# Four cross-attention layers on one core: a narrow job's sixteen heads of scores in one group of plain float32 products, into four PSUM banks

## The chip, the cores and the metric

The kernel runs on one core of one Trainium2 chip. The metric is the device time of one execution in microseconds; three executions of a kernel are shown and their median is what is compared. One more execution was recorded by the hardware profiler, and all rows below come from it. TensorE (PE in the rows) multiplies, VectorE (DVE), ScalarE (ACT) and GpSimd (POOL) work elementwise, SyncE (SP) issues DMAs. PEld is TensorE's loading of the stationary operand.

## The reference, cut to what matters

```python
# x: (8, 128, 128); ctx: (8, 128, 256). Layers 0 and 3 (narrow): 16 heads of width 8 over 4 key/value heads, RMS norm
inv = rsqrt(mean(x * x, -1) + 1e-5)
q = (x * inv * norm_w) @ wq                # (B, T, 16, 8), seen as (B, T, g=4, r=4, 8)
k, v = ctx @ wk, ctx @ wv                  # (B, S, g=4, 8)
attn = softmax(einsum('btgrd,bsgd->bgrts', q, k) / sqrt(8))
x = x + einsum('bgrts,bsgd->btgrd', attn, v).reshape(B, T, 128) @ wo
# Layers 1 and 2 (wide): 16 heads of width 64, own keys and values per head, no norm
logits = einsum(q, k) * 64 ** -0.5 + col_bias       # two or four columns suppressed by a mask
x = x + softmax(logits) @ v @ Wo + bo
```

The result must agree with float32 arithmetic. A product of float32 operands runs on TensorE as two instructions ("hi" and "lo" passes over the same columns; every such matmul appears twice in the counts). Operands of type float32r run in one pass at lower precision; where the kernel before uses them, it splits a number into a rounded part and a rest and sums three products.

## The kernel before

**Jobs and halves.** A job is one layer for one of the eight batches: 32 jobs, in the order of `JOBS`. Jobs 0 to 3, 12 to 15, 16 to 19 and 28 to 31 are narrow (layers 0, 3, 0, 3), the sixteen others wide. Each job has two halves, o = 2n + h, of eight heads ("octet"), and each octet two sides of four heads, one PSUM bank of 128 x 512 each. All engines step through the same halves, each with a hand-written order (`half` in each block): in half o, TensorE makes the scores of octet o, transposes the probabilities of octet o-2, multiplies the values of octet o-3, makes the products of the context that the table `FILLS` names for this half (keys and values of later jobs, one bank each), the queries of the next job and, in even halves, the output projection of job n-2. VectorE reads the scores and writes them negated with a running minimum (L615, four instructions per side), takes reciprocals of the sums (L622), copies transposed probabilities (L626) and outputs (L631, L633) out of PSUM. ScalarE takes the exponentials (L482, four per side), copies one side's transposes in narrow jobs (L499), and copies every fill (L468) and the wide queries (L474). GpSimd normalises (L379).

**Banks.** Two banks `scores_ps`, two `pt_ps` for transposes, two `fill_ps` used in turn by all fills (`fill_bank`), one `v_ps` (values, output, mean square), one `q_ps` (queries). A half's scores can be written only when VectorE has read those of the half before; from octet 57 on, after the last fill, the odd octets take the two fill banks instead (`scores_bank`).

**A narrow job's scores.** The four key heads of width 8 stand as 32 rows; `diagonal_keys` (L334) spreads them into a block form of 4 x 128 columns, so that one product of 512 columns gives four heads' scores. Precision comes from a stack of three such parts (`STACK` = 96 rows): rounded query with rounded key, rest of the query, rest of the key, in float32r, one pass. `queries` (L788) makes the stacked query for four r's by four products; `narrow_queries` on VectorE rounds it (L594) and takes the rest (L598), both over 512 columns; `split_keys` on GpSimd (`first_keys_rest` on VectorE for the first) rounds the keys. `scores` (L825) then runs two products of 512 columns in each half.

**Things that the steps touch.** `fill_out` on ScalarE copies a fill after `exponentials(o, 1)`, in half o for the first name of a half and at the start of half o+1 for the second. `weighted_values` waits for `rms_out` of a job whose mean square shares the bank. `mean_out` (L586) is the first step of the narrow norm on VectorE, right after `add_input` at the start of an odd half.

```python
scores:  pe.wait_ge(scores_read[side], m + 1)    # m: the octet before in these banks
         nc.tensor.matmul(out[side][:], qn[0:STACK, n % 2, 2 * h + side, :], keys, ...)
```

## Time and profile before

| | us |
|---|---|
| three runs, median (lowest to highest) | 380.88 (380.61 to 384.76) |
| the profiled execution's own time | 380.89 |
| its span, first to last instruction | 379.1 |
| TensorE / VectorE / ScalarE / GpSimd busy | 359.7 / 267.7 / 279.0 / 187.6 |

The profiled execution lies within 0.01 us of the median, and 1.79 us of it lie outside the span. Narrow jobs' scores are made from 10.1 to 48.3, from 159.6 to 235.5 and from 333.3 to 366.1 us; between these stretches lie the wide jobs.

### The profile page before, as it was taken

The page shows a single profiled execution, that of the slowest core. Times are in us where ns is not written, and L with a number is a line of the kernel's source. Part 1 is how long each engine was busy: PE and PEld are TensorE (multiplying, and loading weights), DVE is VectorE, ACT ScalarE, POOL GpSimd, SP SyncE. Part 2 cuts the span into 40 slices and gives each one's busy share as a digit, 9 for nine tenths or more (in the row PEclk, how much of TensorE's full clock was granted, in tenths as well). Part 3 has the DMA queues.
Part 4 walks back from the last instruction along what each step waited for, and adds up shares of the span by engine and source line. Part 5 has one row for each costly group of instructions (what it writes and reads, how often), then busy time and mean ns, then how long its engine had stood idle before and what let it go on. Part 6 is the DMA issues. An engine that isn't in the chain of part 4 may idle for free.

```text
span 379.1 us, 10494 instructions
## 1 busy us (share of the span) xinstructions
PE 359.7 (95%) x3522; PEld 319.1 (84%) x3522; DVE 267.7 (71%) x1401; ACT 279.0 (74%) x1176; POOL 187.6 (49%) x220
## 2 busy tenths in 40 slices
PE   8889999999999999999999999999999999978665
PEld 8787799899999998889889988888999989867554
DVE  2999975636536547696978886577564785699982
ACT  4889998865665567475899999998566865647793
POOL 3677853733223236454676765443333435447662
PEclk9899999999999999999999999999999999999979
DMA  7925000000000000000000000000000000000000
GB/s 232 411 66 216 1 3 3 2 3 2 1 2 3 2 0 3 2 3 0 10 3 9 9 8 2 3 3 2 0 3 2 3 2 1 2 3 3 7 9 14
DMA packets 4883, 9.91 MB, mean 26 GB/s; under 512 B 608, under 2 KB 3296, under 8 KB 4576
## 3 DMA queue, kind: packets, MB, share of 16 engines
q1 hardware_dynamic: 4400, 8.91, 6.5%
q8 instruction: 29, 0.48, 0.5%
q10 hardware_dynamic: 432, 0.34, 0.4%
q14 instruction: 22, 0.18, 0.2%
HBM read 8.73 MB, written 0.52 MB: 24 GB/s over the span
## 4 chain that ended last, share of the span: by engine, by line
PE 74%; DVE 21%; ACT 3%; issue 1%; DVEq 0%; POOL 0%; POOLq 0%
PE pt_ps L849 13%; PE scores_ps L836 9%; DVE probs L615 8%; PE q_ps L796 8%; PE fill_ps L701 7%; PE v_ps L900 7%; PE v_ps L882 7%; PE fill_ps L702 7%; PE fill_ps L703 7%; PE v_ps L870 3%; DVE probsT L626 3%; ACT probs L482 3%; PE q_ps L788 2%; DVE qn L598 2%; DVE qn L594 2%; PE scores_ps L825 2%
## 5 line engine op out<-in xcount | busy, mean ns | idle before, releaser
L482 ACT ACTIVATE probs<-probs,negmax 128x128 f32<-128x128 f32 x512 | 198.5, 391 | 81.0 <-DVE negmax L615 80.9
L379 POOL TENSOR_TENSOR probs<-probs,inv 128x512 f32<-128x512 f32 x128 | 137.3, 1075 | 176.8 <-DVE inv L622 176.4
L482 ACT ACTIVATION_READ_ACCUMULATOR probs<-probs,negmax 128x1 f32 x512 | 96.8, 189 | 0.0
L615 DVE CUSTOM_DVE_ANT_0 probs<-scores_ps,col_bias 128x128 f32<-128x128 f32 x256 | 58.2, 284 | 39.1 <-PE scores_ps L836 39.1
L849 PE MATMUL pt_ps<-smalls,probs 128*128 128x128 f32 x512 | 70.5, 282 | 6.2 <-DVE probsT L626 6.2
L849 PEld LDWEIGHTS pt_ps<-smalls,probs 128*128 128x128 f32 x512 | 57.6, 143 | 18.2 <-issue 14.8
L615 DVE CUSTOM_DVE_ANT_0 probs<-scores_ps,no_bias,inv_rms 128x128 f32<-128x128 f32 x224 | 64.2, 343 | 5.8 <-PE scores_ps L825 5.4
L626 DVE COPY probsT<-pt_ps 128x512 f32<-128x512 f32 x96 | 63.0, 684 | 2.6 <-PE pt_ps L849 0.5
L615 DVE DVE_READ_ACCUMULATOR2_ANT negmax<- 128x1 f32 x512 | 42.5, 83 | 0.0
L701 PE MATMUL fill_ps<-c_hi,w_hi 128*128 128x256 f32 x128 | 38.3, 300 | 0.0
L836 PE MATMUL scores_ps<-kT,qT 64*128 64x128 f32 x512 | 37.2, 285 | 0.0
L882 PE MATMUL v_ps<-probsT,v 128*64 128x128 f32 x512 | 35.0, 279 | 1.6 <-DVE rms L586 1.0
L702 PE MATMUL fill_ps<-c_hi,w_lo 128*128 128x256 f32 x128 | 36.1, 282 | 0.0
L703 PE MATMUL fill_ps<-c_lo,w_hi 128*128 128x256 f32 x128 | 36.0, 281 | 0.0
L836 PEld LDWEIGHTS scores_ps<-kT,qT 64*128 64x128 f32 x512 | 31.1, 187 | 3.9
L796 PE MATMUL q_ps<-x,w_qo 128*128 128x128 f32 x256 | 34.0, 276 | 0.0
L882 PEld LDWEIGHTS v_ps<-probsT,v 128*64 128x64 f32 x512 | 27.4, 136 | 7.1 <-issue 4.0
L796 PEld LDWEIGHTS q_ps<-x,w_qo 128*128 128x128 f32 x256 | 31.9, 191 | 1.3 <-issue 0.4
L900 PE MATMUL v_ps<-oT,w_qo 128*128 128x128 f32 x256 | 31.7, 277 | 0.0
L643 DVE SCALAR_TENSOR_TENSOR x<-v_ps,smalls,x 128x128 f32<-128x128 f32 x16 | 5.6, 347 | 35.3 <-PE v_ps L900 35.3
L900 PEld LDWEIGHTS v_ps<-oT,w_qo 128*128 128x128 f32 x256 | 29.9, 192 | 0.0
L701 PE MATMUL fill_ps<-w_hi,c_hi 128*128 128x512 f32 x64 | 27.5, 430 | 0.3 <-ACT v L468 0.3
(92 smaller groups left out, 583.2 us busy)
## 6 DMA issues: line engine op xcount, KB each, us to landing
kT<-in_kv_w SPq DMA_DIRECT2D x6, 512.0 KB, 6.4
w_qo<-in_qo_w SPq DMA_DIRECT2D x2, 1024.0 KB, 8.3
v<-in_ctxT SPq DMA_DIRECT2D x4, 256.0 KB, 9.5
v<-in_kv_w SPq DMA_DIRECT2D x2, 512.0 KB, 11.2
outT<-x SPq DMA_DIRECT2D x8, 64.0 KB, 1.6
wn<-in_narrow_w SPq DMA_DIRECT2D x2, 192.0 KB, 5.7
x<-in_xT SPq DMA_DIRECT2D x1, 384.0 KB, 8.1
oT<-in_narrow_kv ACTq DMA_DIRECT2D x1, 256.0 KB, 3.9
```

What stands on the lines that cost most here:

```text
L379: nc.gpsimd.tensor_tensor(p4, p4, inv[:, o % 2, side, :].unsqueeze(2).broadcast_to([P, 4, S]), ALU.mult,).then_inc(probs_made[side], 1)
L482: last = nc.scalar.activation(e, e, ACT.Exp, scale=-1.0, bias=negmax[:, o % 2, side, q:q + 1], accum_out=rowsum[:, o % 2, side, q:q + 1])
L615: last = nc.vector.tensor_tensor_reduce(out=probs[:, o % PROBS_RING, side, cols], in0=banks[scores_bank(o)][side][:, cols], in1=bias, scal ...
L626: nc.vector.tensor_copy(probsT[:, o % PROBST_RING, side, :], pt_ps[side][:]).then_inc(pt_read[side], 1)
L701: nc.tensor.matmul(out, a_hi, b_hi, start=(n == 0), stop=False)
L702: nc.tensor.matmul(out, a_lo, b_hi, start=False, stop=False)
L703: last = nc.tensor.matmul(out, a_hi, b_lo, start=False, stop=(n == len(moving) - 1))
L796: last = nc.tensor.matmul(q_ps[:, c * T:(c + 1) * T], w_qo[:, l - 1, first:first + P], x[:, b, :], start=True, stop=True)
L836: last = nc.tensor.matmul(out[side][:, c * S:(c + 1) * S], qT[rows, 4 * h + c, :], kT[rows, f % KV_RING, 4 * h + c, b % 2 * S:(b % 2 + 1) ...
L849: last = nc.tensor.transpose(pt_ps[side][:, cols], probs[:, o % PROBS_RING, side, cols], identity)
L882: last = nc.tensor.matmul(v_ps[side * WIDE_D:(side + 1) * WIDE_D, c * T:(c + 1) * T], v[:, f % KV_RING, b % 2, head * WIDE_D:(head + 1) * ...
L900: last = nc.tensor.matmul(y_ps, w, oT[:, c, :], start=(c == 0), stop=(c == (1 if l in NARROW else IC) - 1))
```

## The change

The stack of three parts goes. Query and key stay float32: the 32 rows of keys are repeated four times (128 rows, one copy per r), one query product of 128 columns gives all sixteen heads, one VectorE instruction scales it, and four float32 products of 32 rows each, one per row group of the array, write four banks: all sixteen heads at once, in the even half. The second octet's banks are the former fill banks. The fills go to whichever of the five banks (scores A0, A1, fill B0, B1, query Q0) the new table names. Waits on banks are counted per bank. The odd half's fill in front of a narrow job is copied by ScalarE before `exponentials(o, 1)`. VectorE waits for transposes of octet o-3 before an odd narrow octet.

```diff
-NQ, NO = 0, 2 * REP * STACK
-NK, NV = 0, 2 * CC * STACK
+NQ, NO = 0, 2 * C
+NK, NV = 0, 2 * CC * P
 FILLS = {
-    0: ["vn0"], 1: ["k0.0", "kn1.0"], 2: ["k0.1", "k0.2"], 3: ["k0.3", "v0.0"], 4: ["vn1", "v0.1"],
-    5: ["v0.2", "bias"], 6: ["v0.3", "k1.0"], 7: ["k1.1", "k1.2"],
...
-    24: ["v3.3"], 25: ["k4.0", "kn2.0"], 26: ["k4.1", "vn3"], 27: ["k4.2"], 28: ["k4.3"], 29: ["v4.0", "kn3.0"],
-    30: ["v4.1", "v4.2"], 31: ["v4.3"], 32: ["k5.0", "k5.1"], 33: ["k5.2"], 34: ["k5.3", "v5.0"], 35: ["v5.1"],
-    36: ["v5.2", "v5.3"], 37: ["k6.0"], 38: ["k6.1", "k6.2"], 39: ["k6.3", "v6.0"],
...
+    0: [("vn0", Q0)], 1: [("k0.0", A0), ("kn1.0", Q0)], 2: [("k0.1", A0), ("k0.2", Q0)], 3: [("k0.3", A1), ("v0.0", Q0)],
+    4: [("vn1", A0), ("v0.1", Q0)], 5: [("v0.2", A1), ("bias", Q0)], 6: [("v0.3", A0), ("k1.0", A1)],
+    7: [("k1.1", A0), ("k1.2", B0)],
...
+    24: [("v3.3", A0)], 25: [("k4.0", A1), ("kn2.0", Q0)], 26: [("k4.1", A0)], 27: [("k4.2", A1), ("vn3", Q0)],
+    28: [("k4.3", A0)], 29: [("v4.0", A1), ("kn3.0", Q0)], 30: [("v4.1", A0)], 31: [("v4.2", A1), ("v4.3", Q0)],
+    32: [("k5.0", A0)], 33: [("k5.1", A1), ("k5.2", Q0)], 34: [("k5.3", A0)], 35: [("v5.0", A1), ("v5.1", Q0)],
+    36: [("v5.2", A0)], 37: [("v5.3", A1), ("k6.0", Q0)], 38: [("k6.1", A0)], 39: [("k6.2", A1), ("k6.3", B0)],
...
+def scores_bank(o, side):
+    return 2 * (o % 2) + side if is_narrow(o // 2) else side
...
 # GpSimd
-            def split_keys(name):
...
             def diagonal_keys(n):
-                pool.wait_ge(kn_split, order + 1)
+                pool.wait_ge(bank_read[FILL_BANK[name]], count_of(FILL_BANK[name], name))
...
 # ScalarE, half
                 if scalar_copy(o - 2):
...
+                soon = h == 1 and is_narrow(n + 1)
+                for name, bank in FILLS.get(o, [])[:1]:
+                    if soon:
+                        fill_out(name)
                 if valid(o):
                     exponentials(o, 1)
-                for name in FILLS.get(o, [])[:1]:
-                    fill_out(name)
+                for name, bank in FILLS.get(o, [])[:1]:
+                    if not soon:
+                        fill_out(name)
...
 # VectorE
-            def first_keys_rest():
...
             def mean_out(n):
                 dve.wait_ge(ms_full, narrow_index(n) + 1)
+                dve.wait_ge(qn_full, narrow_index(n) + 1)
...
             def narrow_queries(n):
-                nc.vector.tensor_scalar(all_parts, q_ps[0:STACK, :], -NARROW_SCALE, None, ALU.mult).then_inc(qn_hi_made, 1)
...
-                nc.vector.scalar_tensor_tensor(
-                    out=rest, in0=q_ps[low, :], scalar=-NARROW_SCALE, in1=rest.bitcast(F32),
...
+                nc.vector.tensor_scalar(qn[:, n % 2], qn_ps, -NARROW_SCALE, None, ALU.mult).then_inc(qn_made, 1)
 
             def scores_out(o, side):
+                if l in NARROW and h == 1 and side == 0 and o >= 3:
+                    for i in range(2):
+                        dve.wait_ge(pt_full[i], o - 2)
+                bank = scores_bank(o, side)
+                dve.wait_ge(bank_full[bank], count_of(bank, (o, side)))
...
 # VectorE, half
                 if h == 1 and is_narrow(n + 1):
                     mean_out(n + 1)
+                    narrow_queries(n + 1)
...
-                for m in NARROW_JOBS:
-                    if m > 0 and query_half(m) == o - 1:
-                        narrow_queries(m)
...
 # TensorE
+            def free_bank(bank, use):
+                if count_of(bank, use) > 1:
+                    pe.wait_ge(bank_read[bank], count_of(bank, use) - 1)
...
-                    for r in range(REP):
-                        first = NQ + (NARROW.index(l) * REP + r) * STACK
-                        last = nc.tensor.matmul(q_ps[0:STACK, r * T:(r + 1) * T], wn[:, first:first + STACK], x[:, b, :],
-                                                start=True, stop=True)
...
+            def narrow_queries(n):
...
+                nc.tensor.matmul(ms_ps, x_sq[:, n % 2, :], mean_w[:, 0:2], start=True, stop=True).then_inc(ms_full, 1)
...
+                nc.tensor.matmul(qn_ps, wn[:, first:first + C], x[:, b, :], start=True, stop=True).then_inc(qn_full, 1)
 
+            def narrow_scores(n):
+                i = narrow_index(n)
+                for r in range(REP):
+                    free_bank(r, (2 * n + r // 2, r % 2))
+                pe.wait_ge(kd_made, i + 1)
+                pe.wait_ge(qn_made, i + 1)
+                for r in range(REP):
+                    rows = slice(PART * r, PART * (r + 1))
+                    nc.tensor.matmul(banks[r][:], qn[rows, n % 2, :], kd[rows, i % KD_RING].rearrange("p g k -> p (g k)"),
+                                     start=True, stop=True).then_inc(bank_full[r], 1)
...
             def weighted_values(n, h):
                 if is_narrow((o + 4) // 2):
                     pe.wait_ge(rms_out, narrow_index((o + 4) // 2) + 1)
+                    pe.wait_ge(qn_made, narrow_index((o + 4) // 2) + 1)
...
 # TensorE, half
-                if valid(o):
-                    scores(n, h)
+                if is_wide(n):
+                    wide_scores(n, h)
+                if is_narrow(n) and h == 0:
+                    narrow_scores(n)
...
                 if h == 0 and is_narrow(n + 1):
-                    mean_squares(n + 1)
+                    narrow_queries(n + 1)
```

Each narrow query weight shrinks from 384 to 128 columns, the narrow key and value weights grow from 512 to 640 columns in one DMA, and the wide jobs keep their scores in A0 and A1, their fills in B0 and B1 and their queries in Q0.

## Rows read from the trace of the kernel before

**Rows 1.** The page, part 1: busy time of each engine
```profile
PE 359.7 (95%) x3522; PEld 319.1 (84%) x3522; DVE 267.7 (71%) x1401; ACT 279.0 (74%) x1176; POOL 187.6 (49%) x220
```
**Rows 2.** Windows: length; PE, PEld, DVE, ACT, POOL busy (x count); clock; DMA share; GB/s
```profile
10.00:48.30 38.30, 34.32 (x277) 29.44 (x277) 36.31 (x162) 34.25 (x132) 29.08 (x29) 0.96 0.44 167
...
59.60:153.80 94.20, 94.20 (x949) 85.62 (x949) 53.07 (x299) 62.24 (x262) 35.14 (x36) 1.00 0.01 2
...
190.00:230.00 40.00, 40.00 (x374) 34.91 (x373) 34.10 (x183) 36.78 (x158) 28.28 (x40) 1.00 0.02 7
...
327.40:353.00 25.60, 21.64 (x198) 18.07 (x198) 24.14 (x115) 15.71 (x75) 15.08 (x21) 1.00 0.01 2
353.00:379.10 26.10, 16.59 (x192) 12.70 (x191) 17.06 (x90) 17.21 (x79) 12.32 (x15) 0.86 0.04 11
```
**Rows 3.** Timeline of PE over one narrow job (start, length, instructions merged)
```profile
207.06 0.71 PE L825 MATMUL scores_ps<-kd,qn 96*128 96x512 f32 x2
207.61 1.04 PE L849 MATMUL pt_ps<-smalls,probs 128*128 128x128 f32 x8
...
209.90 1.03 PE L788 MATMUL q_ps<-x,wn 128*96 128x128 f32 x8
210.69 0.71 PE L825 MATMUL scores_ps<-kd,qn 96*128 96x512 f32 x2
...
216.50 0.48 PE L825 MATMUL scores_ps<-kd,qn 96*128 96x512 f32 x1
```
**Rows 4.** Timeline of PE where parts of the array are used, 240 to 244
```profile
240.72 1.16 PE L836 MATMUL scores_ps<-kT,qT 64*128 64x128 f32 x16
241.81 1.09 PE L849 MATMUL pt_ps<-smalls,probs 128*128 128x128 f32 x8
242.84 1.08 PE L870 MATMUL v_ps<-probsT,v_narrow 128*32 128x128 f32 x32
```
**Rows 5.** Groups by line and form: busy us, mean ns of one
```profile
L482 ACT ACTIVATE probs<-probs,negmax 128x128 f32<-128x128 f32 x512 | 198.5, 391 | 81.0 <-DVE negmax L615 80.9
...
L796 PE MATMUL q_ps<-x,w_qo 128*128 128x128 f32 x256 | 34.0, 276 | 0.0
...
L598 DVE SCALAR_TENSOR_TENSOR qn<-q_ps,qn 32x512 fp32r<-32x512 f32 x16 | 10.9, 683 | 0.6
L594 DVE TENSOR_SCALAR qn<-q_ps 96x512 fp32r<-96x512 f32 x16 | 10.8, 676 | 0.0
...
L631 DVE COPY oT<-v_ps 128x128 f32<-128x128 f32 x16 | 4.6, 289 | 3.4 <-PE v_ps L870 3.3
...
L738 PE MATMUL fill_ps<-qT,mean_w 128*128 128x512 f32 x2 | 1.0, 592 | 0.0
```
**Rows 6.** Timeline of the first scores, all engines
```profile
7.45 0.42 DVE L578 TENSOR_TENSOR kn<-fill_ps,kn 32x256 fp32r<-32x256 f32 x1 [0.16 <-ACT kn L444]
...
10.09 0.70 PE L825 MATMUL scores_ps<-kd,qn 96*128 96x512 f32 x2 [0.21 <-DVE qn L598]
...
11.52 0.35 DVE L615 CUSTOM_DVE_ANT_0 probs<-scores_ps,no_bias,inv_rms 128x128 f32<-128x128 f32 x1
```
**Rows 7.** Waits from 10 to 55: total us, times, longest
```profile
ACT probs L482 <- DVE negmax L615: 4.0, 5, 1.3
```
**Rows 8.** Timeline of ACT: the first exponential after the scores at 207.06
```profile
208.82 0.40 ACT L482 ACTIVATE probs<-probs,negmax 128x128 f32<-128x128 f32 x1 [0.75 <-DVE negmax L615]
```
**Rows 9.** Timeline where narrow jobs give way to wide ones, twice
```profile
53.74 1.16 PE L836 MATMUL scores_ps<-kT,qT 64*128 64x128 f32 x16
...
54.63 0.59 ACT L468 ACTIVATE kT<-fill_ps 128x512 f32<-128x512 f32 x1
...
240.79 0.58 ACT L468 ACTIVATE kT<-fill_ps 128x512 f32<-128x512 f32 x1
```
**Rows 10.** Timeline of PE near the end
```profile
360.04 1.20 PE L825 MATMUL scores_ps<-kd,qn 96*128 96x512 f32 x2
361.73 1.94 PE L849 MATMUL pt_ps<-smalls,probs 128*128 128x128 f32 x8 [0.49 <-DVE probsT L626]
```

227 lines of the change are left out of this document (95 added, 132 removed), and 6 rows, old and new, of the table FILLS.

## The prediction

> **What bounds the kernel now.** I read the busy times first: TensorE works 95% of the span, the next engine 74% [rows 1]. A share over the whole span hides stages, so the windows come next [rows 2]. In the wide stretch 59.6 to 153.8 TensorE is busy without a gap, VectorE 56%, ScalarE 66%: this is TensorE's alone. In the narrow stretch 190 to 230 it is also full, but ScalarE has 36.8 of 40 us and VectorE 34.1. In the first narrow stretch (10 to 48.3) VectorE leads with 36.3 of 38.3 us, and TensorE has 4 us of idle time. In the last (327.4 to 353) VectorE has 24.1 of 25.6 us; after 353 nobody is full, the jobs hang on one another. So TensorE work saved counts only in the middle jobs (12 to 19), and VectorE work saved only in jobs 0 to 3 and 28 to 31. Then comes one narrow job on TensorE [rows 3]: starts tell more than lengths, since matmuls overlap. From one even half's scores to the next are 216.50 - 207.06 = 9.44 us. Of these the query products (L788) hold the queue for 210.69 - 209.90 = 0.79, and each half's pair of score products for 207.61 - 207.06 = 0.55.
>
> **The change on TensorE.** Removed per narrow job: 0.79 + 2 x 0.55 = 1.89 us. Added: one query product of two passes, 2 x 0.11 = 0.22 (L788's eight passes hold 0.79, a tenth each; a little is added for the change of kind). And four float32 products of 512 columns, two passes each. Such a pass isn't in this form in the trace; the nearest are the bias product, 592 ns for 512 columns, and L796, 276 ns for 128 [rows 5]. 384 columns more cost 0.316 us, so 512 columns stream in 0.42 to 0.43. If the four row groups work at the same time, the eight passes hold the queue for 2 x 0.43 = 0.86; one after another they hold it for 3.4. Which it is the trace tells only by neighbours [rows 4]: the wide scores use half the rows per product, and 16 passes hold the queue for 1.09 us, from 240.72 to 241.81, where 8 passes over the whole array are listed with the same 1.09; the narrow values use a quarter of the columns, and 32 passes take 1.08. So two row groups and four column groups run side by side. I take four row groups as side by side too. Going into and out of such a group costs: 16 passes in pairs should hold as long as L788's eight, 0.79, and hold 1.09, that is 0.30 more. Scores: 0.86 + 0.30 = 1.16. A job: 1.89 - 1.16 - 0.22 = 0.51 saved; bounds -2.0 (all in turn) and +0.8 (no switching cost).
>
> For this the Trainium skill (TensorE: Matmul & The Clock Gate, "Measured speedup vs the span model") has a figure: four row tiles of 512 columns ran 3.07 times as fast, not four times. By that the eight passes would hold 3.41 / 3.07 = 1.11 us instead of 0.86, if its figure holds none of the switching that I count apart, and the forecast would be 8 x 0.25 = 2 us later. Rows 4, with two row groups, neither confirm nor refute it.
>
> **The first stretch (jobs 0 to 3).** On VectorE a job loses L594 and L598, 0.68 each, and gets one instruction over 128 columns, nearest row L631 at 0.29 [rows 5]: 1.07 less. For job 0 the keys' rest at 7.45 (0.42) goes too, and with it the wait in front of the block form of the keys; the first scores are made at 10.09 and read at 11.52 [rows 6]. I take 1.2 us for this start: VectorE reaches c_lo that much earlier. Jobs 1 to 3 give 3.2 more, together 4.4. But ScalarE takes over: it waited for VectorE only 4.0 us in 10 to 55 [rows 7], so no more than that can come out. I take 3.0. The shared DMA of narrow keys and values grows by a quarter, that of the queries falls to a third; I take nothing for both, within 0.3 either way.
>
> A new wait costs some of it. At half 8 the wide scores need bank A0, which now holds fill k1.1 of half 7, and ScalarE copies that only after `exponentials(7, 1)`. Before, the scores started at 53.74 while that copy ran from 54.63 to 55.2 [rows 9]: 1.5 us late. Behind the waiting scores stands all of TensorE's queue. ScalarE will have moved forward too, so I take 0.8. The stretch gives 3.0 - 0.8 = 2.2; bounds 0.5 and 3.9.
>
> **The middle (jobs 12 to 19).** 8 x 0.51 = 4.1 us of TensorE's queue. What is late next is ScalarE. Its busy time per job is 36.78 / 40 x 9.44 = 8.68 us. There is also a loop that did not exist: even half's scores, VectorE, exponentials, and then the copy of the fill in A1, for which the next even half's scores wait. Before, the first exponential came 208.82 - 207.06 = 1.76 us after the scores began [rows 8]; now the first bank is full only after 1.15 instead of 0.55 us, so 2.35. From there to the end of the A1 copy ScalarE has its job's 8.68 less one set of exponentials (4 x 0.39 = 1.54 [rows 5]) and less one fill copy (0.5): 6.65. Loop: 2.35 + 6.65 = 9.0 and a semaphore, against TensorE's own 9.44 - 0.51 = 8.93. So 0.1 per job is lost: 0.8. At half 25 the wide values of job 11 stand directly behind an output projection and wait for VectorE's add, mean and query scaling, about 0.5; against this, 0.7 of stalls in front of VectorE in this stretch should go. At half 40 the wide scores need A1 (fill k6.2 of half 39), copied after the exponentials that ended at 240.79, when the scores had begun at 240.72 [rows 4, 9]: copy and semaphore, 0.6. Sum: 4.1 - 0.8 - 0.5 + 0.7 - 0.6 = 2.9; bounds -0.5 and 4.7. Moving fills to other halves changes no count.
>
> **The wide stretches** keep their instructions and their two fill banks: nothing, within 0.3. GpSimd loses the key splits and was idle half the time: nothing.
>
> **The end (jobs 28 to 31).** VectorE is the bound up to 353 [rows 2], and 4 x 1.07 = 4.3 us of its work goes, the last of it at 356. Two things come back. The old tail gave odd octets other banks, so TensorE made octet 62's scores at 360.04 without waiting for octet 61. Now all four banks must be read first, at about 360.9, then 1.2 us of scores, and only then the transposes, which started at 361.73 [rows 10]: 0.5 late. And in each even half VectorE has 0.85 us of other work to hide 1.25 us of scores: 0.2 of it shows. The granted clock averages 0.86 after 353 [rows 2]; the transposes at 361.73 took 1.94 us at the lower level, 1.2 GHz, against 1.09 for the same eight at full clock [rows 4, 10]. The scores could fall into such a time and cost 1.0 more; I keep that for the range. The end gives 4.3 - 0.5 - 0.2 = 3.6; bounds 1.2 and 4.6.
>
> **Sum.** 2.2 + 2.9 + 3.6 = 8.7. The profiled execution took 380.89 us (span 379.1 and 1.79 around it), 0.01 above the median, so the forecast is 380.9 - 8.7 = 372.2 us.
>
> **Rivals.**
> - *Four row groups don't run together.* The place is the eight passes of `narrow_scores`; the price per job is 0.22 + 0.30 + 3.41 / k, with k the number of groups at work. In the middle it passes the old 1.89 at k = 2.5. For k = 2 a job costs 0.34 more there: 8 x 0.34 + 0.6 of half 40 = 3.3 lost; the later scores take 0.85 of each VectorE saving at both ends, leaving 0.5 and 1.0: 380.9 + 3.3 - 1.5 = 382.7. For k = 1 it is 8 x 2.04 = 16 us in the middle, near 398. For it: no row shows four row groups, or four banks written at once. Against it: rows 4 show exact halving for two and quartering for columns. From k = 2.2 on down the whole is slower. Chance 0.11.
> - *The four-bank waits eat the middle.* All four banks must be free before anything is made, by ScalarE's A1 copy and VectorE's reads. If ScalarE runs 0.4 us later per job than I count, the middle gives nothing after its stalls, and both passages cost their full 1.5 and 0.7: 380.9 - 1.5 - 0.3 - 3.0 = 376.1. For it: ScalarE is 92% busy there. Against it: ScalarE's own sum still fits. Chance 0.22.
> - *More than forecast.* The loop hides behind its neighbours, the passages cost nothing because ScalarE has moved as far as TensorE, and the ends give their whole VectorE work: 3.9 + 4.3 + 4.3 = 12.5, 368.4. Chance 0.15.
> - The forecast, 372.2, has the remaining 0.52.
>
> **Range and chances.** 368.0 to 378.5: it holds the forecast, the second rival and nearly all of the third, and leaves out the first. A measurement tells 1%, 3.8 us, from no change. Faster by more (below 377.1): 0.52 + 0.15 + 0.15 of the second rival's 0.22 = 0.82. Within 1%: the other 0.07 of that rival and 0.03 of the first: 0.10. Slower: 0.08.
>
> **What would show it.** Right: the four scores passes begin within a few hundredths of a us of one another, twice, and the group holds the queue about 1.16; the period of a middle job is 9.0; L594 and L598 are one group of about 0.29; VectorE no longer waits for scores in odd halves; TensorE waits for ScalarE's kT copy in front of the wide scores of halves 8 and 40; VectorE sheds some 17 us of busy time. Wrong: passes 0.43 apart, each to itself; a middle period above 9.2 with TensorE waiting in front of every even half's scores; the first stretch no shorter than before, with ScalarE full; or a tail in which the scores run at the lower clock.

## The result, and the profile after

The changed kernel took 385.87 us (median of 13 runs, 385.09 to 387.20) against 380.92 for the kernel before on the same chip: ratio 1.0118, 95% interval 1.0097 to 1.0140. It is 1.2% slower; 372.2 was forecast, and the range ended at 378.5. The profiled execution took 386.64 us, 0.8 above the median; its span is 384.9 us, 5.8 more than before, and this is what the stretches below add up to.

First the page, part 1, and then windows of the changed kernel (columns as in [rows 1, 2]):

```profile
PE 353.1 (92%) x3490; PEld 304.1 (79%) x3490; DVE 248.2 (64%) x1384; ACT 280.5 (73%) x1176; POOL 179.9 (47%) x206
```
```profile
10.00:48.30 38.30, 32.69 (x274) 25.88 (x273) 32.98 (x158) 35.36 (x136) 28.95 (x28) 0.96 0.43 163
59.60:153.80 94.20, 94.20 (x949) 85.66 (x947) 53.07 (x299) 62.99 (x266) 34.49 (x35) 1.00 0.01 2
190.00:230.00 40.00, 36.37 (x350) 28.98 (x349) 27.50 (x173) 34.69 (x148) 24.54 (x32) 1.00 0.03 8
332.50:358.00 25.50, 19.80 (x187) 15.54 (x190) 20.35 (x111) 16.10 (x76) 14.27 (x20) 0.98 0.00 1
358.00:384.90 26.90, 17.23 (x204) 12.15 (x196) 15.89 (x89) 17.14 (x78) 12.07 (x14) 0.88 0.04 11
```

VectorE shed 19.5 us and TensorE 6.6, and still the span grew. In the middle (190 to 230) all three engines now have gaps, TensorE 3.6 us, where before it had none [rows 2]. Work went and waits came. Where they came shows in four stretches, cut by the same instruction in both kernels: the first scores, the wide scores of halves 8, 23 and 55, and the end. Two of the cuts are new here; the kernel before (L836), then the changed one (L814):

```profile
153.69 0.38 PE L836 MATMUL scores_ps<-kT,qT 64*128 64x128 f32 x2
...
327.41 0.38 PE L836 MATMUL scores_ps<-kT,qT 64*128 64x128 f32 x2
```
```profile
54.65 0.94 PE L814 MATMUL scores_ps<-kT,qT 64*128 64x128 f32 x12 [1.06 <-ACT kT L458]
...
153.97 0.49 PE L814 MATMUL scores_ps<-kT,qT 64*128 64x128 f32 x4
...
332.53 0.38 PE L814 MATMUL scores_ps<-kT,qT 64*128 64x128 f32 x2
```

| stretch | before | after | difference | forecast |
|---|---|---|---|---|
| first scores (10.09; 10.10) to half 8 | 43.65 | 44.55 | +0.9 | -2.2 |
| half 8 to 23 (wide) | 99.95 | 99.32 | -0.6 | 0 |
| half 23 to 55 (mixed, middle, wide) | 173.72 | 178.56 | +4.8 | -2.9 |
| half 55 to the end | 51.7 | 52.4 | +0.7 | -3.6 |

The 0.6 us of the wide stretch are in half 22, the last before the cut, where job 12's query product is made: the step to half 23 took 7.42 us and takes 6.78. The forecast had this in the middle.

Part of the +4.8 is the clock's in this one execution. From job 14's scores to job 15's the changed kernel takes 11.44 us, with the clock at its lower level for 3.4 us of it. The kernel e3 further down, whose one edit doesn't touch these halves, takes 9.87 for the same step at full clock. Windows, of the changed kernel and then of e3:

```profile
182.60:194.04 11.44, 10.01 (x86) 7.64 (x87) 6.83 (x42) 8.46 (x38) 6.13 (x9) 0.85 0.03 8
```
```profile
181.64:191.51 9.87, 8.43 (x86) 6.86 (x87) 6.74 (x42) 8.46 (x38) 6.13 (x9) 1.00 0.03 9
```

So 1.6 of the 4.8 us are the clock's. Of the runs below, e2 (11.62) and e4 (11.50) have the lower clock in this step too, the others have not. Whether the unprofiled executions had it is not known.

Next the arithmetic itself. TensorE's timeline over one middle job of the changed kernel (to be laid beside [rows 3]):

```profile
203.90 0.70 PE L797 MATMUL scores_ps<-kd,qn 32*128 32x512 f32 x2 [0.74 <-issue]
203.91 0.70 PE L797 MATMUL fill_ps<-kd,qn 32*128 32x512 f32 x2
204.40 0.62 PE L797 MATMUL scores_ps<-kd,qn 32*128 32x512 f32 x2
204.44 0.59 PE L797 MATMUL fill_ps<-kd,qn 32*128 32x512 f32 x2
204.97 1.09 PE L827 MATMUL pt_ps<-smalls,probs 128*128 128x128 f32 x8
...
208.66 0.47 PE L786 MATMUL v_ps<-x,wn 128*128 128x128 f32 x2
208.97 0.39 PE L879 MATMUL v_ps<-oT,wn 128*128 128x128 f32 x2
...
213.77 0.70 PE L797 MATMUL scores_ps<-kd,qn 32*128 32x512 f32 x2 [0.71 <-issue]
```

Four passes begin within 0.02 us of one another (203.90, 203.91, two each), the other four half a us later: four row groups do work side by side, and sixteen heads hold the queue for 204.97 - 203.90 = 1.07 us. The query product holds 208.97 - 208.66 = 0.31. So far the forecast (1.16 and 0.22) stands. But the period is 213.77 - 203.90 = 9.87, not 9.0, and ahead of every even half's scores TensorE stands 0.7 us. VectorE and ScalarE in the same job:

```profile
206.34 0.40 ACT L473 ACTIVATE probs<-probs,negmax 128x128 f32<-128x128 f32 x1 [0.53 <-DVE negmax L597]
...
209.39 0.29 DVE L623 TENSOR_TENSOR x<-v_ps,x 128x128 f32<-128x128 f32 x1 [1.04 <-PE v_ps L879]
...
211.06 0.40 ACT L473 ACTIVATE probs<-probs,negmax 128x128 f32<-128x128 f32 x1 [0.56 <-DVE negmax L597]
...
212.62 0.57 ACT L490 ACTIVATE probsT<-pt_ps 128x512 f32<-128x512 f32 x1
...
213.09 0.57 ACT L458 ACTIVATE kT<-scores_ps 128x512 f32<-128x512 f32 x1
```

Read it backwards from 213.77: the scores need bank A1, ScalarE copies its fill at 213.09 to 213.66, behind the copy at 212.62, behind the odd octet's exponentials at 211.06. Those waited 0.56 for VectorE, which had stood 1.04 until 209.39 for the output projection, though the odd octet's scores lay ready from 204.97. The sum over this stretch is in the waits of the changed kernel, 190 to 230 (total, times, longest):

```profile
DVE probs L597 <- PE scores_ps L797: 8.4, 4, 2.1
ACT probs L473 <- DVE negmax L597: 5.5, 8, 1.6
...
DVE x L623 <- PE v_ps L879: 4.1, 4, 1.0
```

VectorE waits 2.1 us per job for new scores: made all at once, they come only when all of the old ones are read. This wait alone is no loss: e7, which is faster than the kernel before, has 8.5 us of it in its own 190 to 230. The loss lies in the loop that it closes with the waits for the output projection and for bank A1, and the experiments are about whether that loop can be shortened.

### The profile page after: what moved, and what is told of

It reads as the page before. It is cut to its first block, busy times and chain, and to the rows that moved or that the text cites. A ratio compares the mean times of both kernels' runs of the same rounds, so it can differ in the third digit from the quotient of the medians.

```text
span 384.9 us, 10406 instructions
## 1 busy us (share of the span) xinstructions
PE 353.1 (92%) x3490; PEld 304.1 (79%) x3490; DVE 248.2 (64%) x1384; ACT 280.5 (73%) x1176; POOL 179.9 (47%) x206
## 4 chain that ended last, share of the span: by engine, by line
PE 81%; DVE 10%; ACT 3%; issue 3%; DMA 1%; SPq 0%; POOL 0%; DVEq 0%; POOLq 0%
PE pt_ps L827 14%; PE scores_ps L814 9%; PE v_ps L879 8%; PE v_ps L861 8%; PE q_ps L766 7%; DVE probs L597 6%; PE scores_ps L797 4%; PE fill_ps L680 4%; PE v_ps L849 4%; PE fill_ps L681 4%; PE fill_ps L682 4%; PE scores_ps L680 3%; PE scores_ps L682 2%; PE scores_ps L681 2%; ACT probs L473 2%
## 5 line engine op out<-in xcount | busy, mean ns | idle before, releaser
L827 PE MATMUL pt_ps<-smalls,probs 128*128 128x128 f32 x512 | 71.6, 284 | 2.4 <-DVE probsT L608 2.4
L597 DVE CUSTOM_DVE_ANT_0 probs<-scores_ps,no_bias,inv_rms 128x128 f32<-128x128 f32 x128 | 36.8, 345 | 23.0 <-PE scores_ps L797 23.0
L814 PE MATMUL scores_ps<-kT,qT 64*128 64x128 f32 x512 | 37.2, 285 | 2.3 <-issue 1.2
L597 DVE CUSTOM_DVE_ANT_0 probs<-fill_ps,no_bias,inv_rms 128x128 f32<-128x128 f32 x128 | 36.7, 344 | 0.0
L814 PEld LDWEIGHTS scores_ps<-kT,qT 64*128 64x128 f32 x512 | 31.1, 187 | 6.2 <-issue 1.4
L797 PE MATMUL scores_ps<-kd,qn 32*128 32x512 f32 x64 | 19.7, 688 | 13.2 <-DVE negmax L597 4.7
L604 DVE RECIPROCAL inv<-rowsum 128x4 f32<-128x4 f32 x128 | 22.1, 173 | 2.9 <-ACT probs L473 2.8
L464 ACT ACTIVATE qT<-q_ps 128x512 f32<-128x512 f32 x32 | 18.7, 583 | 6.6 <-PE q_ps L766 6.6
```

The lines of the kernel that those rows point to most:

```text
L597: last = nc.vector.tensor_tensor_reduce(out=probs[:, o % PROBS_RING, side, cols], in0=banks[bank][:, cols], in1=bias, scale=scale, scalar= ...
L797: nc.tensor.matmul(banks[r][:], qn[rows, n % 2, :], kd[rows, i % KD_RING].rearrange("p g k -> p (g k)"), start=True, stop=True).then_inc(b ...
L814: last = nc.tensor.matmul(banks[side][:, c * S:(c + 1) * S], qT[rows, 4 * h + c, :], kT[rows, f % KV_RING, 4 * h + c, b % 2 * S:(b % 2 + 1 ...
L827: last = nc.tensor.transpose(pt_ps[side][:, cols], probs[:, o % PROBS_RING, side, cols], identity)
```

## The experiments

Fourteen kernels; each ratio is to the kernel before, run beside it (381.0 to 381.4 us). The four stretches are cut as above; the period is one step from an even half's scores to the next in the steady part of the middle. Such steps of one kernel differ by up to 0.08 us, so 9.07 and 9.09 are the same. Times and ratios come from all runs of a kernel, stretches and periods from its one profiled execution.

| run | us | ratio, 95% | to 8 | to 23 | to 55 | end | period |
|---|---|---|---|---|---|---|---|
| e1 | 383.96 | 1.0066 (1.0031-1.0101) | 45.7 | 99.3 | 174.1 | 53.1 | 9.39 |
| e2 | 389.13 | 1.0209 (1.0157-1.0260) | 45.2 | 99.3 | 179.3 | 56.2 | 10.04 |
| e3 | 383.72 | 1.0077 (1.0044-1.0111) | 44.1 | 99.3 | 175.7 | 52.4 | 9.86 |
| e4 | 389.07 | 1.0203 (1.0153-1.0253) | 45.6 | 99.3 | 178.6 | 56.1 | 9.86 |
| e5 | 380.25 | 0.9972 (0.9944-1.0001) | 44.8 | 99.3 | 173.1 | 50.5 | 9.20 |
| e6 | 380.57 | 0.9964 (0.9937-0.9991) | 45.3 | 99.3 | 172.8 | 52.0 | 9.39 |
| e7 | 376.62 | 0.9886 (0.9838-0.9934) | 43.4 | 99.3 | 171.2 | 50.6 | 9.07 |
| e8 | 388.53 | 1.0187 (1.0151-1.0223) | 43.4 | 99.3 | 179.6 | 54.3 | 10.51 |
| e9 | 382.54 | 1.0016 (0.9984-1.0048) | 43.4 | 100.0 | 174.1 | 54.5 | 9.44 |
| e10 | 375.52 | 0.9824 (0.9773-0.9875) | 43.6 | 99.3 | 170.5 | 50.1 | 9.09 |
| e11 | 373.73 | 0.9781 (0.9728-0.9834) | 43.6 | 99.3 | 170.5 | 48.5 | 9.08 |
| e12 | 375.51 | 0.9833 (0.9777-0.9888) | 43.6 | 99.3 | 170.1 | 51.3 | 9.08 |
| e13 | 373.67 | 0.9792 (0.9753-0.9830) | 44.1 | 99.3 | 170.3 | 48.6 | 9.07 |
| e14 | 380.67 | 0.9976 (0.9954-0.9999) | 43.7 | 100.0 | 173.7 | 51.1 | 9.44 |

**e1: the A1 fill ahead of the transposed probabilities.** In ScalarE's `half`, the copy of `FILLS[o][:1]` in a half that is `soon` stands ahead of the L490 copy instead of behind it.

> Edit: in the odd half in front of a narrow job ScalarE copies the fill in A1 before it copies the transposed probabilities (L490), no other change. Theory 'hand-over' (the middle's period is a ring: scores, values, fill, output projection, VectorE's add and scores_out(odd), exponentials, L490, copy of A1, next scores): one copy of 0.48 us leaves the ring, so the period of a middle job falls from 9.87 to 9.4 us, 8 jobs give 3 to 4 us, time near 382.5. Rival 'TensorE's own work' (the group of four products with its changes of mode costs more than its slots show): the period stays 9.87, time 385.9. Rival 'B banks' (scores wait for VectorE's reads of the odd octet, not for ScalarE): also unchanged.

```profile
201.51 0.70 PE L797 MATMUL scores_ps<-kd,qn 32*128 32x512 f32 x2 [0.26 <-issue]
...
210.90 0.70 PE L797 MATMUL scores_ps<-kd,qn 32*128 32x512 f32 x2 [0.23 <-issue]
```

TensorE's timeline: 9.39 from one to the next, and the stall is down from 0.7 to 0.2. The order of two copies on ScalarE moved each job by 0.48, and such a copy holds ScalarE for 0.47 (212.62 to 213.09 in the changed kernel): the loop through ScalarE is the bound of the middle. Of the 4.5 us that the third stretch lost, 1.6 are the low clock that this execution doesn't have there. In all, 1.9 us came and not the 3.4 expected: the first stretch is 1.1 us longer than in the changed kernel, and the end 0.7. The clock averages 0.83 from 30 to 40 us here and 1.00 in the changed kernel, but e10 has the same 0.83 and takes no longer than e11 without it, so why the first stretch grew stays open (e6 shows it too).

**e2: no fill in A1 in the odd halves.** In the table, both fills of a pair of halves that use A0 and A1 go to the even half, the query bank's to the odd one:

```diff
-    28: [("k4.3", A0)], 29: [("v4.0", A1), ("kn3.0", Q0)], 30: [("v4.1", A0)], 31: [("v4.2", A1), ("v4.3", Q0)],
+    28: [("k4.3", A0), ("v4.0", A1)], 29: [("kn3.0", Q0)], 30: [("v4.1", A0), ("v4.2", A1)], 31: [("v4.3", Q0)],
```

> Edit: in halves 24 to 39 the fills of odd halves no longer use A1; even halves fill A0 and A1, odd ones Q0 (B0 at 39), so no scores wait for a copy made in the half before. Theory 'hand-over': the wait for ScalarE in front of the even scores goes; but the output projection now stands behind two fills, 1.5 us later, and VectorE's odd octet after it; its reads of B1 then end the ring: about 6.5 + 0.4 + 0.5 + 2.2 = 9.5 us per job, 3 us less over the stretch, time near 383. The passage at half 40 loses its wait too, 1.3 us less: near 382. Rival 'B banks': the ring is bound by VectorE's reads already, so a later output projection makes it longer, 9.87 or more, time 386 or above.

```profile
204.99 0.70 PE L797 MATMUL scores_ps<-kd,qn 32*128 32x512 f32 x2 [0.91 <-DVE negmax L597]
...
215.04 0.70 PE L797 MATMUL scores_ps<-kd,qn 32*128 32x512 f32 x2 [0.90 <-DVE negmax L597]
```

The period grew to 10.04, and TensorE stands 0.9 us not for ScalarE but for VectorE's reads of the other two banks. With two products ahead of it, the output projection came 1.4 us later (6.48 us behind the scores, not 5.07), VectorE waited 2.08 us for it instead of 1.04 with the odd octet unread, and the loop closed through VectorE instead. Taking one bank out of the loop doesn't help; VectorE's order is behind both. The run also had the lower clock over its last 14 us, to which e11 comes back.

**e3: the early copy at the exits too.** `soon = h == 1 and (is_narrow(n + 1) or is_narrow(n))`.

> Edit: ScalarE copies the first fill of an odd half before exponentials(o, 1) also where the next job is wide (halves 7 and 39, fills k1.1 and k6.2). Theory: TensorE's wide scores of halves 8 and 40 wait for exactly these copies; the stall of 1.2 us at 54.7 and of 1.3 us at 245 go, time 2.4 us less, near 383.5. Rival (ScalarE is full there and only hands the delay on: the exponentials come 0.5 later, and the values behind them): under 0.8 us less.

From the last even narrow scores to the first wide ones it took 11.82 and 10.32 us (53.70 - 41.88, 241.30 - 230.98) against 12.95 and 11.59 in the changed kernel. The 1.1 and 1.3 us are what TensorE stood at 54.65 and 245.10 for ScalarE's copies. The period stayed. The third stretch is 2.9 us shorter than in the changed kernel: 1.3 are this wait, 1.6 the low clock that is absent here.

**e4: the tail in two groups of two.** For jobs 28 to 31, heads' groups 0 and 1 in the even half and 2 and 3 in the odd half:

```diff
-                for r in range(REP):
+                turn = range(2 * h, 2 * h + 2) if split else range(REP)
+                for r in turn:
...
-                if is_narrow(n) and h == 0:
-                    narrow_scores(n)
+                if is_narrow(n) and (h == 0 or n >= 28):
+                    narrow_scores(n, h, n >= 28)
```

> Edit: jobs 28 to 31 make their scores in two groups of two products, A banks in the even half and B banks in the odd one, as the kernel before did; all others as in the change. Theory: the last stretch gained nothing because four banks must be free at once (VectorE's reads of the odd octet, then 1.1 us of scores before the transposes: stalls of 2.5 and 2.3 us before the scores at 357.2 and 366.5); with single octets the VectorE work saved comes out: the stretch from 332.5 to the end falls from 52.3 to about 49.5 us, time near 383. Rival (the end is bound by ScalarE's exponentials and the chain between engines, whatever the banks): the stretch stays within 0.7 us of 52.3.

It got longer: 56.1. Each group of two holds the queue as long as the group of four (1.06 us, 337.90 to 338.96), so a job pays twice, and VectorE's addition still stands ahead of the odd octet. Yet from job 28's first scores to job 31's it took 28.9 us, against 29.4 in the changed kernel; the loss stands behind them. The last 11.5 us were at the lower clock, as the window says:

```profile
378.00:389.50 11.50, 7.50 (x79) 5.46 (x77) 2.63 (x7) 2.07 (x8) 1.35 (x2) 0.50 0.05 13
```

How much of the 3.7 us is the clock's and how much the split's, this run doesn't separate. e2, whose end has the instructions of the changed kernel, lost 3.8 us there with the low clock over its last 14 us, so the clock may be nearly all of it.

**e5: VectorE reads the odd octet first.** In the odd half of a narrow job the waiting work goes behind the ready work:

```diff
+                late = h == 1 and is_narrow(n)
-                if h == 1 and n >= 2:
+                if h == 1 and n >= 2 and not late:
                     add_input(n - 2)
...
                 if valid(o):
                     scores_out(o, 1)
+                if late and n >= 2:
+                    add_input(n - 2)
+                if late and is_narrow(n + 1):
+                    mean_out(n + 1)
+                    narrow_queries(n + 1)
```

> The changed kernel, but in the odd half of every narrow job VectorE reads the odd octet's scores first and only then does the residual addition, the mean and the query scaling, which wait for the output projection. In the changed kernel's end stretch VectorE stood 1.91 us in front of the addition at 354.00 with the odd octet's scores ready since 348.3, read them until 356.8, and TensorE stood 2.37 us in front of the next scores at 357.20. Theory (the end is bound by the order on VectorE, because four banks must be read before anything is made): the stalls of 2.3 to 2.4 us in front of the scores of the last three narrow jobs go, and the stretch from the wide scores of half 55 to the end falls from 52.3 to about 46. In the middle ScalarE's wait of 0.56 in the odd half goes with it, and the period falls from 9.87 to about 9.4. Total about 376 us. Rival (the end is a chain through exponentials, transposes and copies, whatever VectorE's order): the end stays at 50 to 52 and the total at 382 to 385.

One edit gave 5.6 us and brought the kernel back to the old time. (In the profiled executions the third stretch lost 5.5 us, of which 1.6 are the absent low clock.) The changed kernel near the end, and then this one (TensorE's timeline, and of the first also VectorE's row of the wait):

```profile
353.79 1.04 PE L827 MATMUL pt_ps<-smalls,probs 128*128 128x128 f32 x8
...
354.00 0.35 DVE L625 SCALAR_TENSOR_TENSOR x<-v_ps,smalls,x 128x128 f32<-128x128 f32 x1 [1.91 <-PE v_ps L879]
...
357.20 1.22 PE L797 MATMUL scores_ps<-kd,qn 32*128 32x512 f32 x2 [2.37 <-DVE negmax L597]
```
```profile
343.12 0.70 PE L803 MATMUL scores_ps<-kd,qn 32*128 32x512 f32 x2
...
351.20 0.70 PE L803 MATMUL scores_ps<-kd,qn 32*128 32x512 f32 x2 [0.46 <-DVE qn L580]
...
359.20 0.70 PE L803 MATMUL scores_ps<-kd,qn 32*128 32x512 f32 x2 [2.37 <-DVE qn L580]
```

In the changed kernel the two engines stood in turn: VectorE 1.91 us for TensorE with readable scores at hand, then TensorE 2.37 us for VectorE. Now jobs follow at 8.1 and 8.0 us, not 10.1 and 9.3. TensorE still stands 2.37 us ahead of the last scores, but for the query scaling, which VectorE now reaches only behind both reads; what went is VectorE's own 1.91 us of standing. The expectation spoke of the last three jobs; the trace has this wait for two (357.20, and 366.45 with 2.30), and 0.15 us for the one at 347.07. The period of the middle is 9.20, better than the 9.4 expected. But the end gave 1.9 instead of 6: from job 28 to 29 it takes 10.58 now and not 9.99 (e10 says why), and the chain behind the last job's scores takes 19.3 us and not 18.4.

**e6: e1 and e3 together.**

> The changed kernel with the two edits that each helped alone: ScalarE copies the A1 fill ahead of the transposed probabilities, and it does so also in the odd half of the last narrow job of a stretch. If the two stalls are separate, the gains add up: period 9.39 (from 9.87), passages 11.8 and about 10.3 (from 12.95 and 11.59), which is 8 x 0.48 of the middle less what did not show alone, and 2.4 of the passages; the end keeps its 52 to 53 us. Total 380 to 381, no faster than the kernel before (380.9). Rival: the passage's gain was only the same time shifted, then 383 to 384.

Period 9.39 and passages as expected; they add up, since the two stalls are different ones. 380.6 is the old time.

**e7: e1, e3 and e5 together.**

> All three edits on the changed kernel: A1 fill copied ahead of the transposed probabilities, also in the last odd half of a narrow stretch, and VectorE's odd octet ahead of the addition and the query scaling. Theory: every loss that the four banks brought is out, so the saved work of TensorE and VectorE shows: middle period 9.0 to 9.3, passages 11.5 and 10, end about 46; total 370 to 374. Rival (ScalarE, 92% busy in the middle, or the chain at the end, is the bound all the same): 378 to 381.

Period 9.07; 376.6 us is faster than the kernel before, though 2.6 above the upper end of what was expected. Two places remained: the entry into the last jobs and the tail's clock. This is TensorE's timeline at the entry:

```profile
336.82 1.09 PE L867 MATMUL v_ps<-probsT,v 128*64 128x128 f32 x16 [1.78 <-DVE rms L574]
```

**e8: the arithmetic without the banks.** Plain float32 and one query product, but eight heads per half in A0 and A1, and the fills in B0 and B1 in their old halves.

> The arithmetic of the change without its banks: plain float32 scores from one query product in the bank of the outputs, but eight heads at a time in each half, in banks A0 and A1, as before; the context's products alternate between B0 and B1 and are made in the halves of the kernel before, and the tail's odd octets go to B0 and B1. VectorE's order as in the change. Theory (the arithmetic gives, the banks take): TensorE's job is 1.89 less in query and score products and gets 0.22 + 2 x (2 x 0.43 / 2 + 0.30) back, about 0.2 to 0.5 saved, so a middle period of 9.1 to 9.3; the first stretch and the end give their VectorE work, 2 to 4 us together; total 373 to 378. Rival (the arithmetic itself loses, by its own switches between row groups or by the query product behind the rms wait): 383 or more.

My working in this expectation was wrong: two row groups take as long as four, so the time of the passes must not be halved. The trace of this run:

```profile
201.38 1.13 PE L798 MATMUL scores_ps<-kd,qn 32*128 32x512 f32 x4 [0.17 <-issue]
202.44 0.33 PE L828 MATMUL pt_ps<-smalls,probs 128*128 128x128 f32 x1
...
208.17 1.13 PE L798 MATMUL scores_ps<-kd,qn 32*128 32x512 f32 x4
209.23 0.44 PE L828 MATMUL pt_ps<-smalls,probs 128*128 128x128 f32 x2
```

Each half's group holds 1.06, against 0.55 before, so a job pays 2.12 + 0.31 for what cost 1.89, 0.54 more. The period grew by 1.07, to 10.51, with TensorE 39.5 of 40 us busy. The other half of it stands at the groups' borders: the even half's scores start 0.43 us after the last product ahead of them (0.15 of it a wait), the odd half's 0.32 us. In all 7.1 us are lost against the kernel before beside it. The new arithmetic pays only when the four groups run together, and for that it needs four banks. The four banks without the new arithmetic were not tried.

**e9: the order of e5 in the kernel before.** `add_input` and `mean_out` behind `scores_out(o, 1)`, where the job before is narrow too.

> The kernel before, with the order on VectorE that helped the changed kernel: in the odd half of a narrow job with a narrow job ahead of it, the odd octet's scores are read before the residual addition and the mean. Theory (the order matters because four banks must be read before anything new is made, so it is worth little where each half has its own pair): the middle stays at 9.44, TensorE's own work; the end gives at most 1 us, since VectorE has 24.1 of 25.6 us there; total 379 to 381. Rival (the order is a gain of its own and the change gives nothing): total 375 to 377, as with the changed kernel.

No gain (1.0016, the interval holds 1). The order is worth 5.6 us only where four banks wait for it. (The profiled execution's end of 54.5 us is a poor one: its mean clock was 0.977, against 0.986 in the kernel before.)

**e10: e7, but the new order only behind a narrow job.** `late = h == 1 and is_narrow(n) and is_narrow(n - 1)`. In the first job of a stretch, wide values in `weighted_values` wait for the mean's read, and that had been put behind both reads of scores.

> The kernel with all three edits, but VectorE's odd octet goes ahead of the addition only where the job before is narrow too. In the first job of a stretch the wide values of the next half wait for the mean's read (TensorE stood 1.78 us at 336.82 for it, and the step from job 28 to 29 took 10.57 us, against 9.99 with the old order). Theory: that step falls back to 10.0 or below and the steps after it stay at 8.0; the same at the entry of the middle stretch; total 375.3 to 376.0 against 376.6. Rival: the wait moves elsewhere, 376.6 or more.

From job 28 to 29 it now takes 9.99, in e7 10.57, and the kernel 375.5. Its last 15 us (TensorE's timeline, then a window of them):

```profile
358.69 1.06 PE L833 MATMUL pt_ps<-smalls,probs 128*128 128x128 f32 x8 [0.20 <-DVE probsT L608]
362.51 1.73 PE L833 MATMUL pt_ps<-smalls,probs 128*128 128x128 f32 x8 [2.76 <-DVE probsT L608]
364.17 1.94 PE L855 MATMUL v_ps<-probsT,v_narrow 128*32 128x128 f32 x32
```
```profile
358.70:362.10 3.40, 1.05 (x8) 0.81 (x8) 2.76 (x19) 3.40 (x18) 2.23 (x3) 1.00 0.00 0
362.10:365.50 3.40, 2.99 (x36) 2.60 (x40) 0.53 (x3) 2.35 (x10) 2.08 (x2) 0.60 0.08 24
```

TensorE was busy 1.05 of 3.4 us, and in what followed the granted clock averaged 0.60, with transposes at 1.73 instead of 1.06 and values at 1.94 instead of 1.08.

**e11: e10 with a busy tail.**

```diff
+            def fill_time(count):
+                for _ in range(count):
+                    nc.tensor.matmul(q_ps[:, 0:T], mean_w[:], mean_w[:], start=True, stop=True)
...
                 if h == 0 and n >= 2:
                     output_projection(n - 2)
+                fill_time({61: 8, 63: 7, 65: 4}.get(o, 0))
```

> The same as the kernel of the run before it in this batch, and TensorE makes 19 products of 128 columns into the free query bank in three places of the tail where it stood idle (8 in half 61, 7 in half 63, 4 in half 65). In the profile with all three edits the clock was at 1.2 GHz from 355.7 to 359.1 and from 369.3 on, after stretches in which TensorE was busy 0.3 of 1.7 us. Theory (the idle time in front brings the lower clock, and it costs time on the chain): transposes 1.97 to 1.09, scores 0.97 to 0.59, values 1.42 and 1.77 to 1.08, output 0.80 to 0.5, together up to 2.7 us, of which 2 show; 373.5 against its neighbour's 375.5. Rival (the clock falls all the same, or the products stand in the way): no difference, or 0.5 us more.

```profile
358.98 1.73 PE L913 MATMUL q_ps<-mean_w 128*128 128x128 f32 x14
361.91 1.06 PE L833 MATMUL pt_ps<-smalls,probs 128*128 128x128 f32 x8 [1.20 <-DVE probsT L608]
362.90 1.08 PE L855 MATMUL v_ps<-probsT,v_narrow 128*32 128x128 f32 x32
```
```profile
354.00:371.30 17.30, 11.95 (x164) 9.34 (x156) 9.11 (x49) 9.56 (x44) 6.39 (x7) 1.00 0.06 16
```

Products whose result nobody reads fill the wait; the clock stays at 1.00 and transposes and values are at 1.06 and 1.08: 1.8 us less. That the Trainium skill (TensorE: Matmul & The Clock Gate, "Part 1: The HAM clock gate (the "warmup" mystery)") has the clock follow how busy the engine was agrees with this pair. At 373.7 this is 7.4 us faster than the kernel before.

**e12: both A products in the even half, the output projection between them,** with the edits of e10.

> All three edits with another table: in the middle the two context products of a pair of halves go to A0 and A1 in the even half and one to the query bank in the odd half, and TensorE makes mean, query and output projection ahead of the even half's second product. VectorE and ScalarE then get the output projection 1.4 us earlier. Theory (the hand-over to ScalarE still costs 0.1 a job: 9.07 against a TensorE job of 8.93): middle period 8.93 to 9.0, total 0.5 to 1 us less than the neighbour with the old table. Rival (TensorE itself has 9.07 of work, since its slots for mean, query and switches are longer than I counted): period 9.07 again or more, and the mixed halves 24 to 30 are longer as in the earlier run of this table; total 1 us more than the neighbour.

Period 9.08 again. As in e7 and e10, TensorE is busy 40.0 of 40 us from 190 to 230 and the scores start 0.20 us behind the last product of 256 columns (0.21 in e10), so no hand-over is left to save. So 9.08 is TensorE's own work per job, and my 8.93 was short. The time is e10's; the profiled execution had a mean clock of 0.982 to e10's 0.986, with more of the lower level in its tail.

**e13: e11 with VectorE copying the second bank in the first stretch.** `scalar_copy(o)` also asks for `o >= 8`.

> The kernel with the inner order and the busy tail, and in the first stretch (octets 0 to 7) VectorE and not ScalarE copies the second bank of transposed probabilities: ScalarE loses 8 x 0.48 us, VectorE gets 8 x 0.60. From the first scores to the wide scores of half 8 the stretch takes 43.6 us, as before the change (43.65), though VectorE shed 1.07 per job. Theory (after the change ScalarE is late there: TensorE stands 1.65 us in front of scores for its kT and v copies, and it is full from 20 to 30): the stretch falls to 41 to 42.5. Rival (VectorE, 19.6 of 20 us busy from 20 to 40, is still the bound, and the products of the context wait for its reads, 2.4 us): the stretch grows to 45 to 47.

The stretch went from 43.6 to 44.1, no time in all. Both theories missed in size. (e11's clock is full from 30 to 40 us and this one's averages 0.83, but e10 has 0.83 there and 43.6 as well.) VectorE had 19.7 of 20 us from 20 to 40 with the copies and 19.6 without, ScalarE fell from 19.0 to 17.1: the little that moved speaks for VectorE as the later one.

**e14: the busy tail in the kernel before** (5 products in half 61, 7 in 63, 4 in 65).

> The kernel before with products into the free query bank in its tail: 5 between the scores and the transposes of half 61, 7 in half 63, 4 in half 65. In its profile the clock is at 1.2 GHz from 358.3 to 365, and on the chain lie transposes 1.94 twice, scores 1.20 and values 1.79 in it. Theory (the busy tail is a gain of its own, which either kernel can have): the low time goes or shrinks, 0 to 2.5 us less, 378.5 to 381, still 5 above the changed kernel with its edits. Rival (the products stand in front of work that was ready, or come too late, since the clock falls on what went before): 381 to 382.

The mean clock of the span rose from 0.986 to 0.995, and only 0.4 us came back, at the edge of what shows. That fits an old tail in which VectorE is late whatever TensorE's clock (before, it is busy 4.79 of 5 us from 355 to 360), but the run doesn't single this out. So the gain of e11 is not one that the kernel before leaves lying.

## Why the prediction was wrong

The forecast missed by 7.7 us in the stretch with the middle (1.6 of them the clock's), by 4.3 at the end and by 3.1 in the first stretch. Its own sign of being wrong came: a middle period above 9.2 with TensorE waiting in front of every even half's scores.

**TensorE's job: right in its own slots, but not the whole of it.** Removed 1.89, forecast 1.38 for what came; measured 1.07 + 0.31 = 1.38. Yet the period fell only from 9.44 to 9.08, by 0.36 and not 0.51. The rest is in the neighbours: the scores start 0.21 us after the last fill product (e10: 207.23, 207.44) where fill products follow at 0.12, and the transposes behind them hold 1.02, not 0.97. I had counted the switching once, inside the group. A single 512-column pass held 0.50, not 0.43; that this and the counted switching of 0.30 made up the right sum was luck. By the Trainium skill's 3.07 (TensorE: Matmul & The Clock Gate, "Measured speedup vs the span model") the passes alone would hold 1.11 us, an estimate; with 0.30 of switching on top, the case that the prediction priced, the runs speak against it, since the whole group holds 1.07. As a figure for the whole group 1.11 is close. No run makes the four products one after another, so this case has no speed-up of its own to lay beside it; from two row groups to four the time goes from 1.06 (e8) to 1.07.

**The middle: the failing step is the loop of 2.35 + 6.65 = 9.0.** The first part came as forecast (206.34 - 203.90 = 2.44). The second, from the first exponential to the end of the A1 copy, was taken as ScalarE's busy time, as if ScalarE had no further wait in it. (4 x 0.39 is 1.56 and not 1.54; that changes nothing here.) It measured 213.66 - 206.34 = 7.32, for the odd octet's exponentials wait for VectorE, VectorE for the output projection, and this stands on TensorE behind the scores. An error of reading helped: the rows at 207.06 and 216.50 of [rows 3], which I took for even halves, are odd ones. The kernel before shows it:

```profile
206.84 0.47 PE L900 MATMUL v_ps<-oT,wn 128*128 128x128 f32 x2
207.06 0.47 PE L825 MATMUL scores_ps<-kd,qn 96*128 96x512 f32 x1
```

L900 ends an even half, so an odd one begins at 207.06. The period is the same, but the first exponential of [rows 8], with its 0.75 us wait for VectorE, belongs to an odd octet: exactly the wait that I left out of the loop. e1 (9.39), e5 (9.20) and e7 (9.07) take the loop apart, and e2 shows its other branch.

**The passages:** the wait at half 8 (1.06 on TensorE, 0.8 taken) and at half 40 (1.20, 0.6 taken) were where I put them, and e3 takes both away.

**The first stretch: the step "4.4 less, capped at 3.0 by ScalarE's waits" failed.** Of the 1.2 us for the start nothing shows in when the first scores come: 10.10, before 10.09 (9.4 to 10.8 in the fourteen runs). VectorE lost its work, but the stretch holds 43.6 us even with all edits. ScalarE's waits for VectorE went only from 4.0 [rows 7] to 2.8 in the changed kernel. In their place TensorE stands in front of banks: at 19.54, 29.87 and 41.70 ahead of scores (1.11, 0.60, 1.28 us) and at 22.04 and 33.62 ahead of fills that go into score banks (0.34, 0.58). e13 speaks for VectorE, not ScalarE, as the later of the two, by little; which wait would have to go for the 3 us to come was not found.

Something that the prediction had no term for ate part of VectorE's gain. From the first scores to half 8 VectorE was busy 40.46 us before, and 39.07 in e11. A small set-up instruction of VectorE there begins while GpSimd splits weights, and lasts until GpSimd is through; in the kernel before it came just ahead of GpSimd's. Timelines of e11, and then of the kernel before:

```profile
39.26 2.37 POOL L381 TENSOR_TENSOR w_lo<-v,w_hi 128x1024 fp32r<-128x1024 f32 x1
...
39.47 2.19 DVE L554 TENSOR_SCALAR suppress<-smalls 128x2 f32<-128x2 f32 x1
```
```profile
41.91 0.14 DVE L558 TENSOR_SCALAR suppress<-smalls 128x2 f32<-128x2 f32 x1
```

It wrote two columns in both. Another (`wn`, L535) takes 1.71 us in e11 where it took 0.39 before, with a third of the columns. In the changed kernel itself only this second one is drawn out, to 1.72 us. Together they took back 3.4 us in e11; no run moves them, so how much of the stretch they cost is not shown.

**The end: "two things come back", 0.7 us, was the wrong list.** I named the tail's last scores and 0.2 us per even half. What came back is a wait of 2.3 to 2.4 us in front of each of the last two jobs' scores (357.20 and 366.45; the scores at 347.07 wait 0.15): VectorE reads two banks, but only after an addition that waits for TensorE, and TensorE can't refill the first two banks meanwhile. VectorE's saved work was real, and turned into VectorE's waiting. The old order hid this since each half had banks of its own (e9).

**The rivals.** "Row groups don't run together" fell with the first timeline. "The four-bank waits eat the middle" named the mechanism, but as ScalarE being 0.4 us late, and it left the ends their gains; at 376.1 it was 10 us short. No rival had the loop between VectorE and TensorE at both ends and in the middle.

## What to carry to other kernels

When a change lets one engine fill all its buffers at once, draw the whole loop, with every wait in it and not with busy times, and ask of each in-order queue in it whether ready work stands behind work that waits. Here moving three small instructions behind ready ones turned a loss of 1.2% into no loss, and with two edits more into a gain of 1.1%. A part of a change may lose alone and win only with the other, as the arithmetic did here without the banks; try the parts apart before giving up either. And compare stretches only beside their granted clock: 1.6 us of one stretch here were the clock's.

## What the runs showed of the hardware that was not expected

- Plain float32 products on two and on four row groups of 32, each into a bank of its own, hold TensorE equally long: 1.06 and 1.07 us for 512 columns in two passes.
- The lower granted clock moved around from kernel to kernel, at both ends and in the middle: 11.5 us of it at the end of e4, 14 at the end of e2, none in the tail of e11, and 3.4 us between jobs 14 and 15 in the changed kernel, e2 and e4 alone. There it cost 1.6 us (11.44 against 9.87). At the end its removal gave 1.8 us in e11 and 0.4 in the kernel before (e14). Tails are not to be compared without a look at the clock: e2's, 3.8 us longer than the changed kernel's, has the same instructions.
- A small VectorE instruction that begins while GpSimd works can last until GpSimd's instruction ends: 2.19 us for two columns that took 0.14 elsewhere, ending at 41.66 where GpSimd ended at 41.63, and 1.71 us for `wn`, ending at 36.16 where GpSimd ended at 36.08 (e11).
